# An embedding, mixer and expert tower on one core: the stretch between z and the experts rearranged, idle matmuls ahead of the h2n turns

## The chip, the cores and the metric

One NeuronCore of a Trainium2 chip runs the whole kernel in one launch. The metric is the device time of one execution in microseconds (us). TensorE (PE) multiplies and turns (transposes), VectorE (DVE), ScalarE (ACT) and GpSimd (POOL) do the elementwise work, SyncE (SP) issues most of the DMAs.

## The reference

```
h   = embed(x)                          # 32 x 128 ids, table 32000, four cutoffs, D = 256; ids outside give 0
n   = layernorm(h)
x1  = n @ w1.T + w1_b;  xc = silu(depthwise_conv3(x1))
y   = scan(xc): s = s*sigmoid(A) + xc*B;  y = sum(s*C) + D*xc      # 256 channels, 16 states, 128 steps
v   = silu(n @ v1.T + v1_b)
h2  = h + (y * v) @ w2.T + w2_b
n2  = layernorm(h2)
out = h2 + 0.5*shared(n2) + 0.25*(two experts of 8, chosen by token index)
shared(n2) = (silu(n2 @ sw1 + sb1) * (n2 @ sw3 + sb3)) @ sw2 + sb2
expert(n2) = gelu(n2 @ w1[e] + b1[e]) @ w2[e] + b2[e]
```

The expert ids are (11 t + 7919 k) mod 8 for token t, so tokens with the same t mod 8 share both experts.

## The kernel before

The kernel computes in fp32 accuracy with split operands: every matrix is kept as a rounded part (hi) and the remainder (lo), and `three` (L1171) issues three matmuls for one product. The hi half is a cast on ScalarE, the lo half a subtraction on VectorE or GpSimd. Each engine runs its own list of instructions in the written order, with semaphores between them.

Phase A embeds and normalizes 4096 tokens in four groups, projects them to x1 and v, and applies the convolution and silu; the result is turned by TensorE (`x_turn`), and `x_hi_part` (L828, ScalarE) and `x_lo_part` (L1030, VectorE) write the scan's input. The last of these tiles, group 3, u = 3, holds the channels from 128 on, and its turn is issued by TensorE behind q = 0 of the scan (L1264).

The scan is done as matmuls with Toeplitz matrices, 16 channels for each q in 0 to 15. For each q and each of two banks TensorE accumulates, ScalarE copies one part (L861), VectorE adds the other (L1067, `y_done`); TensorE's q waits for the y_done of q - 2. From q = 8 on y is also turned back, and `z_part` (VectorE, L1061) multiplies it into v: that is z. SyncE's Toeplitz loads run through the scan; behind them are queued the loads of h for slots 0 and 1 (`h_load`, into h_in) and the weight pieces (`piece_in(n)`). Pieces 0 to 8 are w2 (0), the experts of slot 0 (1: expert 7 into ex1, 8: expert 0 into ex0) and the six shared matrices sw (2 to 7). `piece_hi(n)` is ScalarE's half of a piece; the other is `piece_lo(n)` of VectorE (2 to 7) or of GpSimd (0, 8), and `first_expert_lo` of GpSimd for the two layers of piece 1.

Between z and the experts, for slot 0, in four groups g of 128 tokens:
- ScalarE makes zc_hi (`zc`, L868), GpSimd zc_lo (`mixer_lo`, L694), TensorE multiplies by w2 (`mixer_mm`);
- VectorE adds h (`mixer_out`, L1080), takes statistics (L985, L989) and adds eps (L994); GpSimd takes the power -1/2 (`power_step`, L563); VectorE writes the normalized h2n (`mixer_norm`, L998);
- TensorE turns h2n (`mixer_turn`, L1293), ScalarE and VectorE write h2nT_hi (L872) and h2nT_lo (L1094).

`add_w2_bias(par, ...)` (GpSimd, L735) adds the mixer's bias to the h of a slot before `mixer_out` uses it. `w2_bank` and `tr2_bank` name the PSUM banks of the mixer products and the turns.

The experts then run in eight slots, each of the 512 tokens with the same t mod 8. A slot has eight units (two of the old expert, four shared, two of the new one): `hidden` is the first layer (12 or 6 matmuls of 512 columns), `second` the second one (12 of 256 columns). Between units 1 and 4 of a slot lie the four `mixer_mm` of the next slot, between 3 and 6 its `mixer_turn`s. In slot 0 the shared units need VectorE's `w_lo_done[0]`: 4 pieces for the first hidden, 6 for the second layer. GpSimd waits for all 6 before it issues the load of the third expert (`expert_in(2, 0)`, L678) and goes into slot 0, whose first instruction is `mixer_lo(1, 0)`. SyncE issues piece 8 when `w_lo_done[1]` is 3, which is the second `first_expert_lo`.

Of the kernel before, what the change touches and what calls it, by code (L numbers as in the profile page):

```python
# [23 lines left out]
P = 128  # L24
# [51 lines left out]
def _tower(nc, ctx, ids, table, small, rows, w_a, w_b, w_e, kernel_rows, h_rows, out):  # L76
# [296 lines left out]
    def y_at(q, bank):  # L373
        first = q * CH + bank * CH // 2
        return y_sb[:, :, first:first + CH // 2]
# [8 lines left out]

    def w2_bank(e, g):

        return ps[(4, 5, 6, 4)[g] if isinstance(e, int) and e == 0 else 6]

    def z_cols(e, g):

# [23 lines left out]
    def _(sp):  # L414
# [9 lines left out]
        def h_load(e, par):  # L424
            sp.dma_start(h_in[:, par, :, :],
                         h_rows[bass.ds(e, 1), :, :, :].rearrange("o p g c -> (o p) g c")).then_inc(h_back[par], 16)
# [14 lines left out]
        def piece_in(n):  # L441
            raw, _, _, signal, _, _, _, src = PIECES[n]
            sp.dma_start(raw, src).then_inc(signal, 16)
# [57 lines left out]
        sp.dma_start(w2_bias, bass.AP(rows.tensor, 0, [[0, P], [D, 1], [1, D]])).then_inc(rows_in, 16)  # L501
        sp.wait_ge(ssm_done, 2 * (TRING - 3))
        h_load(0, 0)
        piece_in(1)
        piece_in(2)
        piece_in(3)
        h_load(1, 1)
        sp.wait_ge(ssm_done, 2 * NQ)
        for n in range(4, 8):
            piece_in(n)  # L510
# [23 lines left out]
    def _(pool):  # L534
# [213 lines left out]
        def first_expert_lo(layer):  # L748

            if layer == 0:  # L750
                pool.wait_ge(w_hi_done, 2)
            nc.gpsimd.tensor_tensor(ex1_lo[:, layer, :], stage[:, 2 + layer, :], f32(ex1_hi[:, layer, :]),
                                    ALU.subtract).then_inc(w_lo_done[1], 1)

        pool.wait_ge(rows_in, 48)
        add_w2_bias(0, 1)
        first_expert_lo(0)
        for g in range(GROUPS):
            mixer_lo(0, g)
        first_expert_lo(1)  # L760
        for g in range(GROUPS):
            power_step(g, g, eps2_done, rstd2_done)
        add_w2_bias(1, 1)
        pool.wait_ge(w_lo_done[0], LO_BY.count(0))
        expert_in(2, 0)
        slot(0, 0, 2)
# [8 lines left out]
    def _(act):  # L775
# [49 lines left out]
            need(act, hn_turned, 4 * i + pair + 1)  # L825
            nc.scalar.copy(hnT_at(hnT_hi, i, pair), hn_bank()).then_inc(hnT_hi_done, 1)

        def x_hi_part(i, u):  # L828
            need(act, x_turned, 4 * i + u + 1)
            nc.scalar.copy(x_at(x_hi, i, u), x_bank()).then_inc(x_hi_done, 1)  # L830

# [24 lines left out]
        run_phase_a(act, {"cat": cat_hi, "emb": h_out, "norm": norm, "hn": hn_hi, "x": x_hi_part, "out": out_, "silu": silu})  # L856

        for q in range(NQ):
            for bank in range(2):
                act.wait_ge(ssm_done, 2 * q + bank + 1)  # L860
                nc.scalar.copy(y_at(q, bank), y_part(q, bank, 1)).then_inc(y_low, 1)  # L861

        def zc(e, g):
            n = GROUPS * e + g
# [28 lines left out]
        def slot(e, par, ahead, before):  # L893
            for n in range(UNITS):
                if ahead and 1 <= n <= 4:
                    zc(e + 1, n - 1)
                if n == 6:

                    nc.scalar.activation(warm_out[:, 1:2], zero[:, :], ACT.Gelu)
                activate(e, n)  # L900
                if n or before:
                    hidden_hi(*((e, n - 1) if n else (e - 1, UNITS - 1)))
                if ahead and 3 <= n <= 6:
                    turn2_hi(e + 1, 1 - par, n - 3)

        piece_hi(1)
        for g in range(GROUPS):
            zc(0, g)
            if g < 2:
                piece_hi(2 + g)  # L910
        nc.scalar.activation(warm_out[:, 1:2], zero[:, :], ACT.Gelu)
        for g in range(GROUPS):
            turn2_hi(0, 0, g)
            piece_hi(4 + g)
        piece_hi(8)
        slot(0, 0, True, False)
        with act.Fori(0, 3) as i:
            slot(2 * i + 1, 1, True, True)
# [6 lines left out]
    def _(dve):  # L925
# [101 lines left out]
            nc.vector.tensor_tensor(hnT_at(hnT_lo, i, pair), hn_bank(), f32(hnT_at(hnT_hi, i, pair)),  # L1027
                                    ALU.subtract).then_inc(hnT_lo_done, 1)

        def x_lo_part(i, u):  # L1030
            need(dve, x_hi_done, 4 * i + u + 1)
            nc.vector.tensor_tensor(x_at(x_lo, i, u), x_bank(), x_at(x_hi, i, u), ALU.subtract).then_inc(x_lo_done, 1)

# [30 lines left out]
        for q in range(NQ):  # L1064
            for bank in range(2):
                dve.wait_ge(y_low, 2 * q + bank + 1)
                nc.vector.tensor_tensor(y_at(q, bank), y_part(q, bank, 0), y_at(q, bank), ALU.add).then_inc(y_done, 1)  # L1067
            if q > NQ // 2:
                z_part(q - NQ // 2 - 1)
        z_part(NQ // 2 - 1)  # L1070
# [68 lines left out]

        for u in range(8, 16):  # L1140
            z_part(u)
        piece_lo(2)
        piece_lo(3)
        for g in range(GROUPS):
            mixer_out(0, 0, g)
            if g >= 1:
# [3 lines left out]
                turn2_lo(0, 0, g - 2)  # L1150
        mixer_norm(0, 0, 3)
        turn2_lo(0, 0, 2)
        piece_lo(4)
        turn2_lo(0, 0, 3)
        piece_lo(5)
        piece_lo(6)
        piece_lo(7)
        slot(0, 0, True, False)
        slot(1, 1, True, True)
        slot(2, 0, True, True)  # L1160
# [9 lines left out]
    def _(pe):  # L1170
# [76 lines left out]
        for q in range(NQ):  # L1247
# [19 lines left out]
            if q >= NQ // 2:  # L1267
                if q == NQ // 2:
                    pe.wait_ge(y_done, NQ)
                y_turn(q - NQ // 2)  # L1270

        def mixer_mm(e, g):
            n = GROUPS * e + g
            need(pe, zc_lo_done, n + 1)
            if isinstance(e, int) and e == 0:
                need(pe, h2_done, g - 2)
            else:
                need(pe, h2_done, n)
            for k in range(HALVES):
                last = three(w2_bank(e, g)[:, 0:D], zc_hi[:, g, k, :], zc_lo[:, g, k, :],  # L1280
                             w2_hi[:, k, :], w2_lo[:, k, :], k == 0, k == HALVES - 1)
            last.then_inc(w2_done, 1)
# [88 lines left out]
        for g in range(GROUPS):  # L1371
            mixer_mm(0, g)
        for g in range(GROUPS):
            mixer_turn(0, g)
        slot(0, 0, True, False)
        with pe.Fori(0, 3) as i:
            slot(2 * i + 1, 1, True, True)
# [59 lines left out]
```

## Time and profile before

| what | value |
|---|---|
| runs shown | 441.69, 441.76, 440.62 us (median 441.69) |
| profiled execution | 440.82 us, span 439.0 us |
| mean granted clock of TensorE | 0.984 |
| busy | PE 400.8, PEld 351.4, DVE 275.9, ACT 243.4, POOL 212.7 us |
| scan on TensorE | 130 to 156.5 us of the span |
| z to the first matmul of slot 0 | 157 to 176.2 us |

Span is from the first to the last instruction. PE is TensorE's matmuls, PEld its weight loads, and the share of busy time is an average over all stages: TensorE is nearly full in the expert slots and half empty between 160 and 176 us.

### The profile page before, as it was taken

The numbers are of one execution on the slowest core, as the hardware profiler recorded it, in microseconds if no ns is written. First come the engines' busy times: TensorE is split into PE (matmuls) and PEld (weight loads), VectorE is DVE, ScalarE is ACT, GpSimd is POOL, SyncE is SP. The second block draws the span as 40 slices with busy tenths as digits, with TensorE's granted clock in tenths as the row PEclk, the third lists the DMA queues.
The fourth block names the chain that finished last, engine by engine and source line by source line (L and its number), as shares of the span: only waits on it lengthen the run. The fifth ranks groups of instructions, "written<-read, shape, count | busy, mean of one in ns | idle before, by whom it ended". The sixth has DMA issues, their size and how long they took to land.

```text
span 439.0 us, 8388 instructions
## 1 busy us (share of the span) xinstructions
PE 400.8 (91%) x2880; PEld 351.4 (80%) x2880; DVE 275.9 (63%) x607; ACT 243.4 (55%) x438; POOL 212.7 (48%) x237
## 2 busy tenths in 40 slices
PE   3879899899998883999999999999999999998996
PEld 2767788788678871788898988988988988887885
DVE  6667998889757689474565565565554654655333
ACT  4567878778876363635535635635635536535442
POOL 7678988831009166558337247247247336433000
PEclk9999999999999897799999999999999999999999
DMA  2533111299959962101111211201301301100101
GB/s 63 156 95 135 49 61 57 70 288 308 299 160 245 255 235 96 50 0 43 52 52 48 55 43 49 73 22 48 95 0 49 96 0 48 48 0 0 49 0 48
DMA packets 32779, 38.86 MB, mean 89 GB/s; under 512 B 3461, under 2 KB 29027, under 8 KB 32624
## 3 DMA queue, kind: packets, MB, share of 16 engines
q1 hardware_dynamic: 29616, 32.99, 24.1%
q0 software_dynamic: 3136, 5.52, 4.4%
q8 instruction: 15, 0.25, 0.2%
q14 instruction: 12, 0.10, 0.1%
HBM read 34.56 MB, written 8.65 MB: 98 GB/s over the span
## 4 chain that ended last, share of the span: by engine, by line
PE 69%; DVE 16%; ACT 6%; issue 5%; POOL 2%; DMA 1%; DVEq 0%; ACTq 0%; POOLq 0%
PE ps L1174 20%; PE ps L1175 20%; PE ps L1176 20%; DVE hid_lo L1107 3%; PE ps L1257 3%; DVE stat L985 2%; PE ps L1293 1%; DVE h2n L998 1%; PE ps L1212 1%; DVE v_sb L1061 1%; PE ps L1259 1%; PE ps L1182 1%; DVE catT_lo L978 1%; DVE act_out L1101 1%; DVE x_mid L1038 1%
## 5 line engine op out<-in xcount | busy, mean ns | idle before, releaser
L1107 DVE SCALAR_TENSOR_TENSOR hid_lo<-act_out,hid_hi 128x512 fp32r<-128x512 f32 x64 | 54.9, 859 | 58.9 <-ACT hid_hi L891 58.9
L878 ACT ACTIVATE act_out<-ps,vec 128x512 f32<-128x512 f32 x32 | 22.1, 689 | 89.7 <-PE ps L1176 89.7
L1101 DVE SCALAR_TENSOR_TENSOR act_out<-ps,vec,act_out 128x512 f32<-128x512 f32 x32 | 24.0, 751 | 53.7 <-ACT act_out L878 53.7
L701 POOL TENSOR_TENSOR h_sb<-h_sb,bias_e 128x256 f32<-128x256 f32 x32 | 24.3, 764 | 53.6 <-DVE h2n L998 53.6
L1176 PE MATMUL ps<-h2nT_hi,sw_lo 128*128 128x512 f32 x128 | 50.0, 391 | 0.0
L1175 PE MATMUL ps<-h2nT_lo,sw_hi 128*128 128x512 f32 x128 | 50.0, 391 | 0.0
L1174 PE MATMUL ps<-h2nT_hi,sw_hi 128*128 128x512 f32 x128 | 49.9, 390 | 0.0
L694 POOL TENSOR_TENSOR zc_lo<-v_sb,zc_hi 128x256 fp32r<-128x256 f32 x32 | 29.2, 912 | 36.5 <-ACT zc_hi L868 36.5
L882 ACT ACTIVATE act_out<-ps,vec 128x512 f32<-128x512 f32 x32 | 22.0, 689 | 41.2 <-PE ps L1176 41.0
L550 POOL DMA_INDIRECT cat<-table_dram,x_ids x32 | 36.6, 1144 | 8.4 <-issue 6.0
L891 ACT ACTIVATE hid_hi<-act_out 128x512 fp32r<-128x512 f32 x64 | 39.7, 622 | 0.0
L1174 PE MATMUL ps<-sw_hi,hid_hi 128*128 128x256 f32 x128 | 37.9, 296 | 1.2 <-DVE hid_lo L1107 1.2
L1174 PE MATMUL ps<-ex_hi,hid_hi 128*128 128x256 f32 x128 | 36.8, 288 | 1.2 <-DVE hid_lo L1107 1.2
L1176 PE MATMUL ps<-ex_hi,hid_lo 128*128 128x256 f32 x128 | 36.2, 283 | 0.0
L1175 PE MATMUL ps<-ex_lo,hid_hi 128*128 128x256 f32 x128 | 36.2, 283 | 0.0
L1176 PE MATMUL ps<-sw_hi,hid_lo 128*128 128x256 f32 x128 | 36.2, 283 | 0.0
L1175 PE MATMUL ps<-sw_lo,hid_hi 128*128 128x256 f32 x128 | 36.1, 282 | 0.0
L1174 PE MATMUL ps<-proj_hi,catT_hi 128*128 128x256 f32 x96 | 30.7, 320 | 3.2 <-DVE catT_lo L978 3.1
L563 POOL TENSOR_TENSOR rstd<-rstd,minus_half 128x1 f32<-128x1 f32 x32 | 18.2, 567 | 26.2 <-DVE rstd L994 25.9
L1176 PEld LDWEIGHTS ps<-h2nT_hi,sw_lo 128*128 128x128 f32 x128 | 24.0, 188 | 5.1
L1174 PE MATMUL ps<-hnT,wv_hi 128*128 128x512 f32 (+1 forms) x64 | 27.5, 430 | 0.6 <-DVE hnT L1027 0.3
L1175 PE MATMUL ps<-proj_lo,catT_hi 128*128 128x256 f32 x96 | 27.8, 290 | 0.0
(134 smaller groups left out, 1258.5 us busy)
## 6 DMA issues: line engine op xcount, KB each, us to landing
toep_l<-kernel_rows_dram SPq DMA_DIRECT2D x14, 512.0 KB, 7.3
toep_r<-kernel_rows_dram SPq DMA_DIRECT2D x12, 512.0 KB, 7.6
h_rows_dram<-h_ring SPq DMA_DIRECT2D x32, 128.0 KB, 2.2
h_in<-h_rows_dram SPq DMA_DIRECT2D x8, 512.0 KB, 4.4
stage<-w_e_dram POOLq DMA_DIRECT2D x7, 512.0 KB, 3.6
out_dram<-o_sb SPq DMA_DIRECT2D x7, 512.0 KB, 3.2
bias_e<-rows_dram SPq DMA_DIRECT2D x1, 1024.0 KB, 6.8
toep_r<-kernel_rows_dram SPq DMA_DIRECT2D x4, 256.0 KB, 6.0
```

The lines of the kernel that those rows point to most:

```text
L550: pool.indirect_dma_start(cat[:, r, :], None, table, bass.IndirectOffsetOnAxis(ap=x_ids[:, i, r:r + 1], axis=0), bounds_check=VOCAB - 1, o ...
L563: nc.gpsimd.tensor_tensor(rstd[:, m:m + 1], rstd[:, m:m + 1], minus_half[:, :], ALU.pow).then_inc(s_rstd, 1)
L694: nc.gpsimd.tensor_tensor(zc_lo[:, g, :, :], z_cols(e, g), f32(zc_hi[:, g, :, :]), ALU.subtract).then_inc(zc_lo_done, 1)
L701: nc.gpsimd.tensor_tensor(at, at, bias_e[:, bass.ds(e, 1), :].rearrange("p o c -> p (o c)"), ALU.add).then_inc(h2_biased, 1)
L878: nc.scalar.activation(act_out[:, n % 4, :], ps[bank][:, :], ACT.Silu, bias=vec[:, C_SB1 + j:C_SB1 + j + 1]).then_inc(act_done, 1)
L882: nc.scalar.activation(act_out[:, n % 4, :], ps[bank][:, :], ACT.Gelu, bias=vec[:, bass.ds(C_B1 + 2 * x + j, 1)]).then_inc(act_done, 1)
L891: nc.scalar.mul(hid_hi[:, n % 4, :], act_out[:, n % 4, :], 0.5 if kind == SHARED else 0.25).then_inc(hid_hi_done, 1)
L1101: nc.vector.scalar_tensor_tensor(act_out[:, n % 4, :], ps[bank + 1][:, :], vec[:, C_SB3 + j:C_SB3 + j + 1], act_out[:, n % 4, :], ALU.add, ...
L1107: nc.vector.scalar_tensor_tensor(hid_lo[:, n % 4, :], act_out[:, n % 4, :], 0.5 if kind == SHARED else 0.25, f32(hid_hi[:, n % 4, :]), ALU ...
L1174: nc.tensor.matmul(out_, hi, rhs_hi, start=start, stop=False, **kw)
L1175: nc.tensor.matmul(out_, hi, rhs_lo, start=False, stop=False, **kw)
L1176: return nc.tensor.matmul(out_, lo, rhs_hi, start=False, stop=stop, **kw)
```

## The change

The diff has six edits.

1. The last x tile's cast and subtraction (group 3, u = 3) move behind the y copies and adds of q = 1. ScalarE still waits for its turn ahead of q = 0.
2. SyncE loads h for slot 1 directly behind h for slot 0, ahead of pieces 1 to 3.
3. GpSimd: the second `add_w2_bias` moves from behind the powers to ahead of the four `mixer_lo`; both `first_expert_lo` move behind the fourth h2n.
4. VectorE: all six `piece_lo` move behind the last `turn2_lo` of slot 0. ScalarE: pieces 1 to 4 behind the four casts of the turns, 5 to 7 after them, piece 8 into unit 1 of slot 0.
5. The fourth mixer product of slot 0 gets bank 3 instead of 4, and TensorE's `mixer_mm` of slot 0 no longer waits for `h2_done`.
6. TensorE issues three 512-column matmuls whose result nobody reads ahead of each of the four turns, and three behind the last.

```diff
-        return ps[(4, 5, 6, 4)[g] if isinstance(e, int) and e == 0 else 6]
+        return ps[(4, 5, 6, 3)[g] if isinstance(e, int) and e == 0 else 6]
...
         h_load(0, 0)
+        h_load(1, 1)
         piece_in(1)
         piece_in(2)
         piece_in(3)
-        h_load(1, 1)
...
         add_w2_bias(0, 1)
-        first_expert_lo(0)
+        add_w2_bias(1, 1)
         for g in range(GROUPS):
             mixer_lo(0, g)
-        first_expert_lo(1)
         for g in range(GROUPS):
             power_step(g, g, eps2_done, rstd2_done)
-        add_w2_bias(1, 1)
+        pool.wait_ge(h2n_done, GROUPS)
+        first_expert_lo(0)
+        first_expert_lo(1)
...
         for q in range(NQ):
+            if q == 0:
+                act.wait_ge(x_turned, 4 * GROUPS)
             for bank in range(2):
                 act.wait_ge(ssm_done, 2 * q + bank + 1)
                 nc.scalar.copy(y_at(q, bank), y_part(q, bank, 1)).then_inc(y_low, 1)
+            if q == 1:
+                x_hi_part(GROUPS - 1, 3, last_one=True)
...
+                if n == 1 and isinstance(e, int) and e == 0:
+                    piece_hi(8)
+
-        piece_hi(1)
         for g in range(GROUPS):
             zc(0, g)
-            if g < 2:
-                piece_hi(2 + g)
         nc.scalar.activation(warm_out[:, 1:2], zero[:, :], ACT.Gelu)
         for g in range(GROUPS):
             turn2_hi(0, 0, g)
-            piece_hi(4 + g)
-        piece_hi(8)
+            piece_hi(1 + g)
+        for n in range(5, 8):
+            piece_hi(n)
         slot(0, 0, True, False)
...
+            if q == 1:
+                x_lo_part(GROUPS - 1, 3, last_one=True)
...
-        piece_lo(2)
-        piece_lo(3)
         for g in range(GROUPS):
             mixer_out(0, 0, g)
...
         turn2_lo(0, 0, 2)
-        piece_lo(4)
         turn2_lo(0, 0, 3)
-        piece_lo(5)
-        piece_lo(6)
-        piece_lo(7)
+        for n in range(2, 8):
+            piece_lo(n)
...
+        def keep_awake(times):
+
+            for _ in range(times):
+                nc.tensor.matmul(ps[2][:, :], w2_hi[:, 0, 0:P], w2_hi[:, :, :], start=True, stop=True)
+
         def mixer_mm(e, g):
             n = GROUPS * e + g
             need(pe, zc_lo_done, n + 1)
-            if isinstance(e, int) and e == 0:
-                need(pe, h2_done, g - 2)
-            else:
+            if not isinstance(e, int) or e:
                 need(pe, h2_done, n)
...
         for g in range(GROUPS):
+            keep_awake(3)
             mixer_turn(0, g)
+        keep_awake(3)
         slot(0, 0, True, False)
```

## Rows read from the trace of the kernel before

**Rows 1.** The profile's page: shares of the chain by engine; one group of DMA issues.
```profile
PE 69%; DVE 16%; ACT 6%; issue 5%; POOL 2%; DMA 1%; DVEq 0%; ACTq 0%; POOLq 0%
...
stage<-w_e_dram POOLq DMA_DIRECT2D x7, 512.0 KB, 3.6
```

**Rows 2.** Windows of 1 us: busy of PE, PEld, DVE, ACT, POOL; clock; DMA share; GB/s.
```profile
150.00:151.00 1.00, 1.00 (x12) 0.94 (x10) 0.88 (x4) 0.43 (x2) 0.00 (x0) 0.51 0.86 249
...
153.00:154.00 1.00, 1.00 (x26) 0.94 (x25) 0.86 (x2) 0.08 (x1) 0.00 (x0) 0.78 1.07 414
...
170.00:171.00 1.00, 0.00 (x0) 0.00 (x0) 0.97 (x4) 0.83 (x2) 0.32 (x1) 0.75 0.03 8
...
180.00:181.00 1.00, 1.00 (x4) 0.66 (x3) 0.00 (x0) 0.35 (x1) 0.56 (x1) 0.63 0.97 332
```

**Rows 3.** Timeline, scan stage: start us, us, instruction [idle before <-releaser].
```profile
133.56 0.19 PE L1257 MATMUL ps<-x_sb,toep_r 128*128 128x64 f16 x1 [0.77 <-DVE y_sb L1067]
...
131.78 0.59 ACT L830 CAST x_sb<-ps 128x512 f16<-128x512 f32 x1 [0.99 <-PE ps L1212]
...
132.26 1.21 ACT L861 COPY y_sb<-ps 128x256 f32<-128x256 f32 x4
...
132.40 0.69 DVE L1032 TENSOR_TENSOR x_sb<-ps,x_sb 128x512 f16<-128x512 f32 x1 [2.44 <-ACT x_sb L830]
...
148.46 0.18 PE L1259 MATMUL ps<-x_sb,toep_r 128*128 128x32 f16 x1 [1.87 <-issue]
```

**Rows 4.** Timeline of VectorE, 163 to 178 us.
```profile
163.26 2.42 DVE L1054 TENSOR_TENSOR sw_lo<-stage,sw_hi 128x512 fp32r<-128x512 f32 x2
165.60 0.41 DVE L1080 TENSOR_TENSOR h_sb<-ps,h_in 128x256 f32<-128x256 f32 x1
...
171.26 0.15 DVE L994 TENSOR_SCALAR rstd<-mv 128x1 f32<-128x1 f32 x1
...
172.07 2.42 DVE L998 TENSOR_SCALAR h2n<-h_sb,mv,rstd 128x256 f32<-128x256 f32 x1 [0.33 <-POOL rstd L563]
...
175.68 0.42 DVE L1094 TENSOR_TENSOR h2nT_lo<-ps,h2nT_hi 128x256 fp32r<-128x256 f32 x1 [0.25 <-ACT h2nT_hi L872]
176.02 1.88 DVE L1054 TENSOR_TENSOR sw_lo<-o_sb,sw_hi 128x512 fp32r<-128x512 f32 x3
```

**Rows 5.** Timeline of GpSimd, 155 to 182 us.
```profile
155.92 2.37 POOL L735 TENSOR_TENSOR h_in<-h_in,bias_row 128x1024 f32<-128x1024 f32 x1 [11.53 <-DMA h_in<-h_rows_dram]
...
164.12 1.00 POOL L694 TENSOR_TENSOR zc_lo<-v_sb,zc_hi 128x256 fp32r<-128x256 f32 x1 [0.29 <-ACT zc_hi L868]
...
171.49 0.55 POOL L563 TENSOR_TENSOR rstd<-rstd,minus_half 128x1 f32<-128x1 f32 x1 [1.17 <-DVE rstd L994]
172.00 2.34 POOL L735 TENSOR_TENSOR h_in<-h_in,bias_row 128x1024 f32<-128x1024 f32 x1
178.20 0.62 POOL L678 DMA_DIRECT2D stage<-w_e_dram  x1 [3.86 <-DVE sw_lo L1054]
180.44 0.87 POOL L694 TENSOR_TENSOR zc_lo<-v_sb,zc_hi 128x256 fp32r<-128x256 f32 x1 [1.62 <-ACT zc_hi L868]
```

**Rows 6.** Timeline of TensorE, 166 to 183 us.
```profile
166.16 0.36 PE L1174 MATMUL ps<-w_hi,zc_hi 128*128 128x256 f32 x1 [1.29 <-DVE h_sb L1080]
...
176.16 0.79 PE L1174 MATMUL ps<-h2nT_hi,ex_hi 128*128 128x512 f32 x1 [0.92 <-DVE h2nT_lo L1094]
...
181.37 0.39 PE L1174 MATMUL ps<-w_hi,zc_hi 128*128 128x256 f32 x1
...
182.18 0.39 PE L1174 MATMUL ps<-h2nT_hi,sw_hi 128*128 128x512 f32 x1
...
182.41 0.40 PE L1175 MATMUL ps<-h2nT_lo,sw_hi 128*128 128x512 f32 x1
```

**Rows 7.** VectorE's halves of pieces by source: ns min/median/max, first and last start.
```profile
L1054 DVE TENSOR_TENSOR sw_lo<-o_sb,sw_hi x4: 676/682/686, 174.7 to 177.2; 128x512 fp32r<-128x512 f32 x4
L1054 DVE TENSOR_TENSOR sw_lo<-stage,sw_hi x2: 1136/1250/1364, 163.3 to 164.3; 128x512 fp32r<-128x512 f32 x2
```

More of the change, by code:

```diff
@@ L826, in hn_hi, with x_hi_part @@
             nc.scalar.copy(hnT_at(hnT_hi, i, pair), hn_bank()).then_inc(hnT_hi_done, 1)
-        def x_hi_part(i, u):
+        def x_hi_part(i, u, last_one=False):
+            if isinstance(i, int) and i == GROUPS - 1 and u == 3 and not last_one:
+                return
             need(act, x_turned, 4 * i + u + 1)
@@ L1028, in hn_lo, with x_lo_part @@
                                     ALU.subtract).then_inc(hnT_lo_done, 1)
-        def x_lo_part(i, u):
+        def x_lo_part(i, u, last_one=False):
+            if isinstance(i, int) and i == GROUPS - 1 and u == 3 and not last_one:
+                return
             need(dve, x_hi_done, 4 * i + u + 1)
```

## The prediction

> **What bounds the kernel now.** The page first: 69% of the chain that ended last is TensorE, 16% VectorE, 6% ScalarE [rows 1]. Most of the kernel is TensorE-bound expert slots, and the change leaves those alone. It works on the three stretches where TensorE is not the bound, so I read the trace in order of time there.
>
> At the start of the scan, TensorE stands idle 0.77 us before its first matmul of q = 2, released by VectorE's y_sb add [rows 3]. Ahead of that add lie ScalarE's x_hi cast (131.78, 0.59 us) and VectorE's x_lo (132.40, 0.69 us) of the last x tile.
>
> From 163 to 176 us VectorE sets the pace. It does two piece halves in 2.42 us, then starts the first mixer add at 165.60, is still at its eps(3) at 171.26, and then its last h2n, an instruction with a tile of 128x256, takes 2.42 us [rows 4]. GpSimd's bias add (172.00, 2.34 us) lies over exactly that stretch [rows 5]. A piece half costs 0.68 us by itself and 1.14 or 1.36 us beside GpSimd's work [rows 7].
>
> From 176.16 TensorE runs twelve matmuls of slot 0 at the low clock: they take until 181.37, where the next two of that width are 0.23 us apart (182.18, 182.41) [rows 6]. The clock fell to half within 170 to 171 us and rose within 180 to 181 us, and an earlier fall lasted from 150 to inside 153 us, after 1.87 us in which TensorE issued nothing [rows 2, 3].
>
> **The change part by part.** I count in the times of the trace before; the gain of the scan's start is taken off at the end.
>
> *Scan start.* The x cast and its subtraction go behind the copies of q = 0 and 1. The first y copy can start at 131.78 in place of 132.26, and the first add no longer stands behind x_lo, which ended at 133.09 [rows 3]. Copy 0.37 us and add 0.42 us (estimates from 1.21 us for four overlapping copies [rows 3] and the 0.41 us of a 128x256 add [rows 4]) give y_done at about 132.6, ahead of 132.8, where TensorE wanted it (133.56 - 0.77). The moved pair costs 0.59 + 0.69 us behind q = 1, under adds that TensorE needs only two q later. Gain 0.77 us if the later stalls keep their length, 0 if they swallow it; I take 0.77, since TensorE's share is 1.00 in the windows at 150 and 153 us, so it works without slack behind it [rows 2].
>
> *Mixer start.* Without the two pieces VectorE's first mixer add moves from 165.60 to 163.3, a gain of 2.3 us. Not all of it is kept: the first power must now wait for GpSimd's last zc_lo (164.12 + 1.00 = 165.12), so power (0.55 us) and h2n(0) come at 165.75, where the old cadence from 163.3 had asked for about 165.3: 0.45 us lost [rows 4, 5]. The fourth mixer matmul no longer waits for an add to free its bank. From the first add to eps(3) were 5.66 us (171.26 - 165.60). So eps(3) comes at 163.3 + 5.66 + 0.45 = 169.4.
>
> *Last h2n.* Before, eps(3) at 171.26 was followed by the power (171.49, 0.55 us) and h2n from 172.07 to 174.49 [rows 4, 5]. GpSimd now has nothing to do between the last power and h2n_done, so h2n costs about 0.40 us (estimate: the add of the same tile takes 0.41), and it ends at 169.4 + 0.81 + 0.40 = 170.6. From its end to the end of the last h2nT_lo were 1.61 us (174.49 to 175.68 + 0.42) [rows 4]; slot 0 starts at 172.3 in place of 176.16. I take 172.1 to 172.3; 3.9 us gained here. GpSimd's first expert half (estimate 1.3 us for 512 columns, between the 0.87 of 256 and the 2.37 of 1024 [rows 5]) starts at 170.65 and is done at 171.95, just in time for the first matmul.
>
> *Idle matmuls.* Five groups of three 512-column matmuls, 0.23 us each at full clock [rows 6]: 0.7 us a group, 1.3 us at half clock. The h2n turns come every 1.4 to 1.5 us (5.66 us for four), so a group fits between two; only the first, right behind the mixer matmuls, can hold a turn, by 0.3 to 0.4 us, and ScalarE and VectorE have that much slack there. The last group lies beside the 1.61 us of turn, cast and subtraction. Cost 0, at most 0.4 us. In return TensorE is idle for no more than 0.8 us at a time up to slot 0; before, it idled 1.29 us ahead of 166.16 [rows 6] and the clock did not fall until 170 us, after three turns with nothing between them. So I expect full clock up to slot 0.
>
> *Bias add and load order.* GpSimd does two adds of 2.37 us ahead of zc_lo(0): 155.92 to 160.6, where zc_lo(0) started at about 160.5 before. The four zc_lo end no later than 165.1, since the last waits for ScalarE anyway [rows 5]. Cost 0 to 0.3 us; if h_load(1, 1), which is now second in the queue, landed only at 160, it would be 1 us.
>
> *Pieces behind.* Here the gain is given back in part. VectorE now has six halves behind the last h2nT_lo where it had three in 1.88 us [rows 4]; GpSimd waits for all six (it waited 3.86 us for the last of them before), then issues its DMA (0.62 us) and only then makes zc_lo of slot 1 (0.87 us), which the mixer matmul in slot 0 needs [rows 5]. Six halves at a cadence of 0.63 us are 3.8 us; the second expert half on GpSimd (about 1.3 us) lies over the first of them, and by the price beside GpSimd that costs 0.6 us [rows 7]. So from 171.95: last half 176.4, DMA issue 176.7 to 177.3 (0.30 us later, as before), zc_lo to 178.2, matmul at 178.2 in place of 181.37 (where zc_lo also ended only at 181.31). TensorE's twelve matmuls in front of it last 2.75 us at full clock, to 174.9. It then stands idle for 3.3 us. Bounds: halves at 0.63 us without any collision 177.6; all at 1.25 us 181.9 [rows 7]. Net gain at this point: 3.2 us.
>
> The expert load of piece 8 leaves later too, behind GpSimd's second half, at about 173.4. With a landing after 3.6 us [rows 1], ScalarE splits it until about 178.1, ahead of the next activation that TensorE's third group needs (178.2 + 0.8 + 2.75). It stays hidden up to some 3 us of delay.
>
> A half beside GpSimd takes nearly twice its time [rows 7], and the one-input h2n waited for nearly the whole add [rows 4, 5]. The Trainium skill (GPSIMD Engine Reference, Specifications) says that GpSimd's SBUF interfaces are shared with VectorE, with contention for instructions in a two-port mode or with two SBUF inputs. By that rule the new order moves a collision from h2n to the first piece half; without a rule of this kind the sum would come out 0.6 us lower, with it as above. The trace agrees.
>
> *The clock after the gap.* 1.87 us of idle TensorE came ahead of a fall that lasted 3.4 us: four windows of 1 us, the first at 0.51 and the last at 0.78 [rows 2, 3], with about half lost in each of the first three and 0.22 in the last, are 1.7 us of full-clock work. The new gap of 3.3 us is nearly twice as long. TensorE is the bound behind it (the shared groups follow one another), so a fall costs about 1.7 us of time; 0 if it doesn't come, 2.5 us if it is like the second, where twelve matmuls took 5.2 in place of 2.75 us [rows 6].
>
> **The sum.** The profiled execution took 440.82 us (span 439.0, and 1.8 around it). 440.8 - 0.8 (scan) - 3.2 (slot 0) + 1.7 (clock) = 438.5. The median of the runs shown is 441.69 and they run from 440.62 to 441.76, so the profiled one is at their lower end; I add 0.4, half the distance: 438.9.
>
> **Rivals.**
> 1. *The clock holds through the gap.* For it: it was full at 165 to 167 us in spite of gaps. Against: once, 1.87 us came ahead of a fall [rows 3]. 438.9 - 1.7 = 437.2.
> 2. *The new gate in slot 0 eats it all (slower).* Place: the mixer matmul of slot 1 behind the first twelve matmuls. If all six halves run at 1.25 us [rows 7], they end at 179.45 and the matmul comes at 181.3, as before; TensorE then idled over 6 us, and the clock falls as the second time, 2.5 us: 440.8 + 2.5 + 0.4 = 443.7, or 442.9 if the scan's 0.8 are kept. It decides from a matmul later than about 180, a half over 1.05 us on average. For it: both halves beside GpSimd were that slow. Against: GpSimd has a single instruction left to run beside them, then waits for them itself.
> 3. *The gain is largely swallowed, no change.* The scan's issue stalls (1.87 us at 146.6 [rows 3]) grow when TensorE comes earlier, h_load lands late, the clock falls for longer: -0.8 becomes 0, -3.2 becomes -2.5, +1.7 becomes +2.5, 441.2 with the 0.4.
>
> **How the numbers follow.** Forecast 0.50, clock holds 0.27, no change 0.15, slower 0.08. A measurement here can tell about 0.3% (1.3 us) from no change: faster is below 440.4, slower above 443.0. The forecast's own range is 437.8 to 440.2; with rival 1 and most of rival 3 the range is 436.5 to 441.3. Faster: 0.50 + 0.27 + a little of rival 3, 0.80; within 0.3% 0.14; slower 0.06.
>
> **What would show it.** TensorE's idle before q = 2 gone; the first mixer add near 162.5, slot 0's first matmul near 171.4 (both with the 0.8 off); no h2n over 0.5 us before slot 0; full clock from 154 us to slot 0; the mixer matmul in slot 0 after about 3.3 us of idle TensorE, released by GpSimd's zc_lo, and a half clock for some 3.4 us around it. Wrong if that matmul comes less than 1.5 us behind the twelfth, or if the clock is low in the stretch of turns, or if the scan ends no earlier.

## The result and the profile after

The changed kernel takes 439.55 us (median of 20 runs, 436.82 to 440.99), the kernel before 441.27 us (20 runs, 440.05 to 443.61). The ratio of the two kernels is 0.995, 95% interval 0.9931 to 0.9969: 2.2 us less, between 1.4 and 3.0 (the two medians are 1.7 us apart). The profiled execution took 438.76 us.

The page of the changed kernel: its span, the clock by slices, the chain's shares and the group of zc_lo subtractions.

```profile
span 437.0 us, 8419 instructions
...
PEclk9999999999999989999999999999999999999999
...
PE 67%; DVE 15%; ACT 5%; issue 5%; DMA 3%; POOL 3%; DVEq 0%; ACTq 0%; POOLq 0%; SPq 0%
...
L694 POOL TENSOR_TENSOR zc_lo<-v_sb,zc_hi 128x256 fp32r<-128x256 f32 x32 | 29.5, 921 | 33.4 <-ACT zc_hi L875 33.3
```

Against [rows 1], DMA's share of the chain has gone from 1% to 3% and POOL's from 2% to 3%, and in the clock line one dip stands in the slice around 158 us where there were two dips, around 148 and from 165 to 187.

The scan's idle ahead of q = 2 is gone: no row of TensorE with idle time stands between 130 and 135 us. What stands there later are three waits with no releaser (timeline of TensorE):

```profile
141.10 0.20 PE L1266 MATMUL ps<-x_sb,toep_l 128*128 128x32 f16 x1 [1.29 <-issue]
...
148.09 0.18 PE L1266 MATMUL ps<-x_sb,toep_r 128*128 128x32 f16 x1 [1.60 <-issue]
...
156.14 0.18 PE L1266 MATMUL ps<-x_sb,toep_l 128*128 128x32 f16 x1 [1.92 <-issue]
```

In this document such a wait is called a stall. Before, the same three stalls were 0.66, 1.87 and 0.39 us, the second of them in [rows 3]; the other two are these:

```profile
141.21 0.21 PE L1259 MATMUL ps<-x_sb,toep_l 128*128 128x32 f16 x1 [0.66 <-issue]
...
155.72 0.18 PE L1259 MATMUL ps<-x_sb,toep_l 128*128 128x32 f16 x1 [0.39 <-issue]
```

Now they are 1.29, 1.60 and 1.92. That is 1.9 us more than before, and the scan's last copies by ScalarE are 0.4 us later (first line before, second line now), not 0.8 us earlier.

```profile
156.53 0.37 ACT L861 COPY y_sb<-ps 128x256 f32<-128x256 f32 x1 [0.16 <-PE ps L1259]
...
156.95 0.37 ACT L866 COPY y_sb<-ps 128x256 f32<-128x256 f32 x1 [0.16 <-PE ps L1266]
```

VectorE from the first mixer add to the last piece half, to be held against [rows 4]:

```profile
164.29 0.41 DVE L1091 TENSOR_TENSOR h_sb<-ps,h_in 128x256 f32<-128x256 f32 x1
...
170.25 0.15 DVE L1001 TENSOR_SCALAR rstd<-mv 128x1 f32<-128x1 f32 x1
...
171.07 0.41 DVE L1005 TENSOR_SCALAR h2n<-h_sb,mv,rstd 128x256 f32<-128x256 f32 x1 [0.33 <-POOL rstd L563]
...
172.42 0.42 DVE L1105 TENSOR_TENSOR h2nT_lo<-ps,h2nT_hi 128x256 fp32r<-128x256 f32 x1 [0.60 <-ACT h2nT_hi L879]
172.76 2.38 DVE L1063 TENSOR_TENSOR sw_lo<-stage,sw_hi 128x512 fp32r<-128x512 f32 x2
175.07 2.48 DVE L1063 TENSOR_TENSOR sw_lo<-o_sb,sw_hi 128x512 fp32r<-128x512 f32 x4
```

The mixer add follows z at once (164.29; z itself ended 1.0 us later than before, when it ended at 163.26), the last h2n takes 0.41 in place of 2.42 us, and the six halves take from 172.76 to 177.55. GpSimd, against [rows 5]: both bias adds at the front, the two expert halves as one row of 3.04 us (1.28 and 1.80), and the DMA issue and zc_lo of slot 1 only behind VectorE's last half.

```profile
156.66 4.69 POOL L735 TENSOR_TENSOR h_in<-h_in,bias_row 128x1024 f32<-128x1024 f32 x2 [12.30 <-DMA h_in<-h_rows_dram]
...
165.15 0.90 POOL L694 TENSOR_TENSOR zc_lo<-v_sb,zc_hi 128x256 fp32r<-128x256 f32 x1 [0.28 <-ACT zc_hi L875]
166.00 0.56 POOL L563 TENSOR_TENSOR rstd<-rstd,minus_half 128x1 f32<-128x1 f32 x1
...
171.56 3.04 POOL L752 TENSOR_TENSOR ex_lo<-stage,ex_hi 128x512 fp32r<-128x512 f32 x2 [0.53 <-DVE h2n L1005]
177.85 0.62 POOL L678 DMA_DIRECT2D stage<-w_e_dram  x1 [3.25 <-DVE sw_lo L1063]
178.50 0.86 POOL L694 TENSOR_TENSOR zc_lo<-v_sb,zc_hi 128x256 fp32r<-128x256 f32 x1
```

TensorE, against [rows 6]. Slot 0 starts at 172.98; its twelfth matmul starts at 175.56, and the next instruction, 3.46 us of idle later, is released by zc_lo:

```profile
170.18 0.44 PE L1303 MATMUL ps<-ident,h2n 128*128 128x128 f32 x2 [0.56 <-DVE h2n L1005]
...
172.98 0.47 PE L1181 MATMUL ps<-h2nT_hi,ex_hi 128*128 128x512 f32 x1 [0.31 <-POOL ex_lo L752]
...
175.56 0.39 PE L1183 MATMUL ps<-h2nT_hi,ex_lo 128*128 128x512 f32 x1
179.41 0.38 PE L1181 MATMUL ps<-w_hi,zc_hi 128*128 128x256 f32 x1 [3.46 <-POOL zc_lo L694]
```

The clock in three stretches (windows: busy of PE, PEld, DVE, ACT, POOL, then the clock, DMA share, GB/s): low while z is turned (before, the same four microseconds were at 1.00), full among the turns of h2n, and full through the idle stretch in this execution.

```profile
157.00:161.00 4.00, 3.71 (x21) 3.33 (x20) 3.55 (x7) 0.76 (x2) 4.00 (x2) 0.57 0.92 306
169.00:173.00 4.00, 2.92 (x14) 1.55 (x12) 3.00 (x11) 3.03 (x8) 2.31 (x4) 1.00 0.01 2
176.00:179.00 3.00, 0.00 (x0) 0.00 (x0) 2.15 (x4) 2.33 (x4) 1.13 (x2) 1.00 0.82 325
```

The mean granted clock differs between the 20 executions: six had 0.996 (mean 437.8 us), three 0.992 (439.0 us), eleven 0.986 or 0.988 (440.2 us). The profiled one is of the first kind. The mean doesn't say where in an execution the clock was low; the profiled one had its fall at 157 us.

### The profile page after: what moved, and what is told of

Its sections match the earlier page's. It is cut to its first block, busy times and chain, and to the rows that moved or that the text cites. A ratio compares the mean times of both kernels' runs of the same rounds, so it can differ in the third digit from the quotient of the medians.

```text
span 437.0 us, 8419 instructions
## 1 busy us (share of the span) xinstructions
PE 401.4 (92%) x2895; PEld 352.5 (81%) x2895; DVE 273.8 (63%) x607; ACT 243.1 (56%) x438; POOL 212.0 (49%) x237
## 3 DMA queue, kind: packets, MB, share of 16 engines
HBM read 34.56 MB, written 8.65 MB: 99 GB/s over the span
## 4 chain that ended last, share of the span: by engine, by line
PE 67%; DVE 15%; ACT 5%; issue 5%; DMA 3%; POOL 3%; DVEq 0%; ACTq 0%; POOLq 0%; SPq 0%
PE ps L1181 20%; PE ps L1182 19%; PE ps L1183 19%; DVE hid_lo L1118 3%; DMA toep_l<-kernel_rows_dram 2%; PE ps L1264 2%; PE ps L1303 1%; DVE stat L992 1%; PE ps L1219 1%; PE ps L1189 1%; DVE sw_lo L1063 1%; DVE catT_lo L985 1%; DVE x_mid L1047 1%; DVE act_out L1112 1%; ACT act_out L885 1%
## 5 line engine op out<-in xcount | busy, mean ns | idle before, releaser
L1183 PE MATMUL ps<-proj_hi,catT_lo 128*128 128x256 f32 x96 | 27.9, 290 | 0.0
```

Of the source, the lines that this page charges most:

```text
L1183: return nc.tensor.matmul(out_, lo, rhs_hi, start=False, stop=stop, **kw)
```

## Experiments

Each was timed against runs of the kernel before on the same chip; its ratio to that kernel is what is compared, since the medians of before lie between 441.0 and 442.3 us.

### e1_gate: GpSimd goes into slot 0 without waiting for VectorE's six halves

```diff
-        pool.wait_ge(w_lo_done[0], LO_BY.count(0))
-        expert_in(2, 0)
         slot(0, 0, 2)
...
             for g in range(2):
                 mixer_lo(1, g)
+                if g == 0:
+                    pool.wait_ge(w_lo_done[0], 2)
+                    expert_in(2, 0)
                 mixer_bias(0, 0, g)
```

> The changed kernel, with one wait of GpSimd moved: it goes into slot 0 with zc_lo of slot 1 at once, and only behind it waits, for 2 of VectorE's piece halves (those of the buffer to be overwritten) in place of all 6, and issues the load of the third expert. Theory (the gate gave back a part of the gain): in the changed kernel TensorE idled 3.46 us ahead of the mixer matmul at 179.41, released by zc_lo. Now zc_lo follows zc_hi (ended 175.90) and the matmul comes about 1.0 us behind the twelfth; 2.4 us less, and about 0.4 to 1.7 us more on average where the clock no longer falls behind the gap: 436 to 437 us against 439.5. Rival (another wait stands right behind, the shared pieces that VectorE halves until 177.5, or ScalarE's wait for piece 8): the idle only moves to the next group and the time is within 0.5 us of the changed kernel, 439 to 440.

Measured 436.71 us (5 runs), ratio 0.9888 (0.9871 to 0.9904). TensorE's first and thirteenth instruction of slot 0:

```profile
173.13 0.47 PE L1182 MATMUL ps<-h2nT_hi,ex_hi 128*128 128x512 f32 x1 [0.31 <-DVE h2nT_lo L1106]
...
177.26 0.39 PE L1182 MATMUL ps<-w_hi,zc_hi 128*128 128x256 f32 x1 [1.15 <-POOL zc_lo L694]
```

The idle stretch is 1.15 us in place of 3.46, and all executions had a mean clock of 0.994 to 0.996. The gate is what it was said to be: in the profiles the mixer matmul stands 12.8 us after the end of z in place of 15.1. It cost the changed kernel about 2.7 us (ratios 0.995 and 0.9888, with 1.1 us of uncertainty). The edit moves the wait behind the first zc_lo and also lowers it from six halves to two; which of the two does more was not separated.

### e2_no_awake: without the fifteen idle matmuls

```diff
         for g in range(GROUPS):
-            keep_awake(3)
             mixer_turn(0, g)
-        keep_awake(3)
```

> The changed kernel without its fifteen idle matmuls. Theory (what they save lies in the shadow of the gate): the clock falls between 169 and 173 us, slot 0's first twelve matmuls take 4 to 5.2 us in place of 2.75, to about 178, but the mixer matmul waits for zc_lo until 179.4 anyway; time within 1 us of the changed kernel (438.5 to 440.5). Rival (the prediction's own step taken alone: the idle matmuls are worth the 2.5 us of the low clock): 441.5 to 442.

Measured 438.20 us, ratio 0.9942 (0.9929 to 0.9955): no slower than the changed kernel, and a little below the range expected. The clock falls among the turns and is back before the mixer matmul (windows, then TensorE's first and thirteenth instruction):

```profile
169.00:176.00 7.00, 5.16 (x14) 3.65 (x14) 5.82 (x11) 4.58 (x9) 3.05 (x3) 0.51 0.31 108
176.00:181.00 5.00, 3.61 (x19) 2.78 (x18) 2.68 (x6) 4.03 (x6) 3.57 (x5) 1.00 0.47 165
```

```profile
171.80 0.79 PE L1181 MATMUL ps<-h2nT_hi,ex_hi 128*128 128x512 f32 x1 [0.92 <-DVE h2nT_lo L1105]
...
178.13 0.39 PE L1181 MATMUL ps<-w_hi,zc_hi 128*128 128x256 f32 x1 [1.39 <-POOL zc_lo L694]
```

Slot 0's twelve matmuls run mostly at half clock and fill the time in which the full clock of the changed kernel only waits: the idle stretch is 1.39 us. The matmul behind it stands 15.2 us after the end of z here (162.9) and 15.1 in the changed kernel (164.3).

### e5_gate_no_awake: both edits

> e1_gate without the fifteen idle matmuls. In e2_no_awake leaving them out cost nothing while the gate stood (438.2 us). Theory (they are worth something only where nothing else holds TensorE behind them): with the gate moved, the twelve matmuls at half clock end about 2.5 us later than in e1_gate, the mixer matmul follows at once, and the time is 1.3 to 2.5 us above e1_gate's 436.7: 438 to 439. Rival (they are worth nothing anywhere, since ScalarE's and GpSimd's chain zc_hi, zc_lo shifts with the first activation and the clock is regained sooner): 436.2 to 437.2.

Measured 437.32 us, ratio 0.9911 (0.9888 to 0.9933), against 0.9888 of e1_gate: 1.0 us more, with intervals that overlap a little. The profiles say the same. The mixer matmul has no idle time ahead of it here:

```profile
178.33 0.39 PE L1182 MATMUL ps<-w_hi,zc_hi 128*128 128x256 f32 x1
```

It stands 14.2 us after the end of z (164.2), where e1_gate has 12.8; the spans are 436.3 and 435.1 us. So with the gate gone the idle matmuls save 1.3 us up to that point, in the one profile of each kernel; the runs put their worth at about 1 us and don't exclude nought.

### e6_fill: thirteen more idle matmuls in the gap

```diff
+                if n == 1 and isinstance(e, int) and e == 0:
+                    keep_awake(13)
                 if ahead and 1 <= n <= 4:
                     mixer_mm(e + 1, n - 1)
```

> The changed kernel with thirteen more idle 512-column matmuls in slot 0, ahead of the mixer matmul that waits for zc_lo: they fill 3.0 of the 3.46 us in which TensorE idled. The gate stays where it was. Theory (in most executions of the changed kernel the clock falls behind this gap: their mean granted clock lies between 0.986 and 0.996, and those at 0.996 take 436.8 to 438.9 us, those at 0.986 to 0.988 take 439.3 to 441.0): the mean clock stays at 0.992 or more in all executions, and the median is 437.5 to 438.2, 1.5 us below the changed kernel. Rival (the falls that cost are those of the scan, and slot 0's costs nothing): 439 to 440 us with clocks spread as before.

Measured 438.08 us, ratio 0.9932 (0.991 to 0.9953), six executions with clocks of 0.991 to 0.996. TensorE in the gap:

```profile
173.86 3.16 PE L1282 MATMUL ps<-w_hi 128*128 128x512 f32 x13
177.46 0.38 PE L1181 MATMUL ps<-w_hi,zc_hi 128*128 128x256 f32 x1 [0.45 <-POOL zc_lo L694]
```

The gate is as late as ever and no useful work was added, yet the lowest mean clocks (0.986 and 0.988) are gone. By medians (438.08 and 439.55) this is worth 1.5 us, by ratios 0.8, and the two intervals overlap. The changed kernel's own executions spread over more: 437.8 us at its highest mean clock, 440.2 at its lowest.

### e3_scan_only and e7_scan_undone: the scan's edit alone, and the change without it

> The kernel before with one edit of the change: the last x tile's cast and subtraction behind the copies and adds of q = 1. Theory (the scan is paced by its issue stalls, which take back what is gained ahead of them): TensorE's idle of 0.77 us before q = 2 is gone, the stalls in the scan grow by about as much (they were 0.66, 1.87 and 0.39 us before, and longer by 0.9 to 1.6 us in the changed kernel), the scan's last matmul ends within 0.5 us of 156.5, and the time is that of before within 0.5 us. Rival (the 0.77 us are kept): scan ends near 155.7 and the time is 0.8 us less.

Measured 440.92 us (12 runs), ratio 1.0002 (0.9988 to 1.0016). The idle before q = 2 was gone, and the three stalls were 1.84, 1.40 and 0.70 us: 3.94 in place of 2.92. The profiled execution has the same span as before, 439.0 us.

> The changed kernel with the last x tile's cast and subtraction back in their old place. Theory (the scan's issue stalls take back what the edit gains, as in e3_scan_only): TensorE's 0.77 us of idle before q = 2 is back and the stalls sum to about 3 us in place of 4.81; the median is that of the changed kernel within 0.5 us (439.0 to 440.0). Rival (the edit gives its 0.77 us here): 440.2 to 440.5 us.

Measured 439.77 us (12 runs), ratio 0.9972 (0.9954 to 0.9989), which overlaps the changed kernel's. The idle of 0.77 us was back, and the stalls 0.66 and 2.15 us, 2.81 in all. So the edit gives nothing that can be told, alone or in the change: what is gained ahead of the first stall goes into the stalls.

This profile shows what the changed kernel's own does not, the fall of the clock behind the gap (TensorE's mixer matmul, then windows):

```profile
177.75 0.58 PE L1171 MATMUL ps<-w_hi,zc_hi 128*128 128x256 f32 x1 [3.40 <-POOL zc_lo L694]
```

```profile
169.00:176.00 7.00, 4.80 (x20) 3.02 (x18) 6.07 (x11) 5.80 (x11) 3.40 (x3) 1.00 0.28 98
176.00:184.00 8.00, 6.25 (x20) 5.25 (x21) 1.67 (x5) 2.88 (x3) 7.21 (x8) 0.57 0.32 114
```

The clock is full through the turns with their idle matmuls, and 0.57 over the eight microseconds from 176, that is some 6.9 us at half clock. TensorE is still idle in the first 1.75 of them, where a low clock costs nothing. What a fall here costs can be read from the mixer matmul to the end of the span. That stretch is 257.6 us in the profiles of before, the changed kernel, e2, e3 and e6, all without a low clock in it. It is 260.2 us here (2.5 more), and 259.2 to 259.3 us (1.6 to 1.7 more) in those of e4, e9, e10 and e11, where the clock was 0.79 over the 8 us from the mixer matmul. The idle time ahead of these falls was 1.8 to 3.4 us; in the changed kernel's profile 3.46 us brought none.

### e9_shift: 24 turns of the identity ahead of the scan

```diff
         pe.wait_ge(h_done, RES * GROUPS)
+        for _ in range(24):
+            nc.tensor.transpose(ps[2][:, 0:P], ident[:, :], ident[:, :])
```

> The changed kernel with 24 turns of the identity more on TensorE in front of the scan (their result is not read): 48 more instructions of TensorE and about 2.7 us. The stalls of the scan without a releaser stood at the same matmul of q = 7, 11 and 15 in the kernel before, in the changed kernel and in three variants with the same instructions ahead of them. Theory (they are waits for TensorE's own instructions, which come in fixed pieces by DMA): each stall now stands 48 instructions earlier in the scan. Rival (they are waits for the scan's data or for buffers): each stall stands at the same matmul as before.

One execution, 443.39 us. Counted over the rows of the scan's 512 matmuls, the stalls of the changed kernel stand in front of the 270th, 384th and 494th, and those of the other twelve profiles stand at the same places (the third where there is one). Here they are in front of the 246th, 360th and 475th: 24, 24 and 19 earlier, where 24 turns with their weight loads had been put in.

```profile
142.64 0.18 PE L1268 MATMUL ps<-x_sb,toep_l 128*128 128x32 f16 x1 [1.14 <-issue]
...
149.77 0.18 PE L1268 MATMUL ps<-x_sb,toep_r 128*128 128x32 f16 x1 [0.90 <-issue]
...
158.26 0.22 PE L1266 MATMUL ps<-x_sb,toep_l 128*128 128x64 f16 x1 [3.10 <-issue]
```

They go with the instructions, not with the data, and not with the time either, since they come 1.5 to 2.1 us later than in the changed kernel (and 0.4 to 1.0 us earlier if one counts from the scan's first matmul, which the turns put back by 2.5 us). The Trainium skill (Runtime: NRT & Kernel Launch, Instruction fetch mechanics) has a sequencer fetch its instructions by DMA in blocks of 256. The trace agrees. In the changed kernel's profile, from the first stall to the second and from the second to the third, the matmuls and weight loads (first two counts) are these:

```profile
141.10:148.09 6.99, 5.39 (x126) 5.31 (x127) 4.12 (x9) 2.61 (x7) 2.95 (x4) 1.00 1.03 237
148.09:156.14 8.05, 5.89 (x127) 5.57 (x126) 5.30 (x11) 2.61 (x7) 0.00 (x0) 1.00 1.03 300
```

That is 253 recorded instructions both times. The Trainium skill calls the cost mostly hidden (same section), and here it was 0.2 to 3.5 us where it showed.

### e10_loads_late and e12_held: fewer bytes on the DMA engines in the scan

> The changed kernel with the loads of h and of pieces 1 to 3 (2 MB) held back until the scan's last matmul. Theory (the scan's stalls, which e9_shift showed to move with the instructions, are long because the DMA engines are full): the first, at 141 us, ahead of these loads, stays at 0.7 to 1.8 us; the third, at 154 to 156 us, is under 0.5 us; the scan ends 1 to 2 us earlier. h arrives about 3 us later than before and the whole takes 2 us or more longer. Rival (the stalls don't depend on these loads): third stall of 0.4 to 1.9 us as before.

One execution, 445.37 us. The stalls were 2.13 and 1.08 us, and there was no third. DMA share (last but one column) in the stretch of the first and ahead of the absent one:

```profile
140.00:145.00 5.00, 2.87 (x59) 2.84 (x59) 1.70 (x4) 1.49 (x4) 4.19 (x6) 0.91 1.05 243
...
150.00:155.00 5.00, 5.00 (x116) 5.00 (x115) 4.28 (x9) 2.61 (x7) 0.00 (x0) 1.00 0.58 147
```

> e8_gate_zc with the loads of pieces 1 to 3 (1 MB) held back until the scan's last matmul; h of both slots is loaded where it was. In e10_loads_late, with h held back too, the third stall was gone, and all came 3 us later for want of h. Theory (the third stall is a price of the DMA load that these pieces are a part of, and the pieces are not needed before 168 us): the third stall is under 0.5 us in the profile, and the time is 0.3 to 1 us below e8_gate_zc's 436.5: 435.5 to 436.2. Rival (the h loads and the Toeplitz loads alone keep the DMA engines full until 155 us, or the stalls' sum stays and only moves to the second): 436.2 to 437.0.

```diff
         h_load(1, 1)
-        piece_in(1)
-        piece_in(2)
-        piece_in(3)
         sp.wait_ge(ssm_done, 2 * NQ)
-        for n in range(4, 8):
+        for n in range(1, 8):
```

(the rest is e8_gate_zc)

Measured 436.85 us (4 runs), ratio 0.9882 (0.9846 to 0.9919), the same as e8_gate_zc. Again there is no third stall, but the other two took 4.97 us:

```profile
142.03 0.20 PE L1266 MATMUL ps<-x_sb,toep_l 128*128 128x32 f16 x1 [2.67 <-issue]
...
150.76 0.18 PE L1266 MATMUL ps<-x_sb,toep_r 128*128 128x32 f16 x1 [2.30 <-issue]
```

The absent third stall proves little, though: the profiles of e1_gate, e4_bias_back, e7_scan_undone and e8_gate_zc lack it too, with all loads in place. The scan of e10_loads_late was 1.0 us shorter than the changed kernel's, as its theory had it, but so was that of e6_fill with all loads in place (25.8 us each, 26.8 in the changed kernel). Over the fourteen profiles the first stall varies from 0.66 to 2.67 us and the second from 0.67 to 3.52. The two with the x tile in its old place have the smallest sums, 2.92 and 2.81 us; the twelve with the edit have 3.15 to 5.14. The first stall shows it best. Counted from the scan's first matmul, TensorE came to it after 10.5 us in the two profiles with the x tile in its old place, and after 9.7 us in the eleven others that have no turns ahead: the edit's 0.8 us has arrived there. The wait ended after 11.2 us in the two, and after 10.8 to 12.4 us (median 11.3) in the eleven. So the gain is gone behind the first stall, as if the instructions came at their own time. That the load of the DMA engines makes the stalls long is not shown, and what sets their lengths stays open. For e12_held the rival held: the time did not fall.

### e4_bias_back: the second bias add back behind the powers

```diff
         add_w2_bias(0, 1)
-        add_w2_bias(1, 1)
...
             power_step(g, g, eps2_done, rstd2_done)
+        add_w2_bias(1, 1)
```

> The changed kernel with the second add_w2_bias of GpSimd put back behind the four powers. Theory (the port shared by VectorE and GpSimd made the last h2n long): the fourth h2n takes about 2.4 us in place of 0.41, slot 0 starts 2.0 us or more later, both expert halves of GpSimd start 2.3 us later, and the mixer matmul behind the gate comes 2 to 2.5 us later; 441.5 to 442 us, the changed kernel's gain gone. Rival (the gate takes it up: VectorE's six halves, not GpSimd, set it, and the collision only moves): less than 1 us more than the changed kernel, 439.5 to 440.5.

Measured 441.36 us (12 runs), ratio 1.0008 (0.9995 to 1.0021). VectorE's last h2n, and GpSimd's add beside it:

```profile
170.40 2.43 DVE L1005 TENSOR_SCALAR h2n<-h_sb,mv,rstd 128x256 f32<-128x256 f32 x1 [0.33 <-POOL rstd L563]
```

```profile
170.33 2.35 POOL L735 TENSOR_TENSOR h_in<-h_in,bias_row 128x1024 f32<-128x1024 f32 x1
```

The h2n is as long as before, and the mixer matmul behind the gate stands 17.1 us after the end of z in place of 15.1. The clock also fell behind the gate's 1.82 us of idle time in this profile (above). With this one move undone, the rest of the change gives nothing that can be told.

### e11_pieces_first: two halves back ahead of the first mixer add

```diff
+        piece_lo(2)
+        piece_lo(3)
         for g in range(GROUPS):
             mixer_out(0, 0, g)
...
-        for n in range(2, 8):
+        for n in range(4, 8):
             piece_lo(n)
```

(with ScalarE's piece_hi(1) to (3) among the first casts, as before)

> The changed kernel with pieces 2 and 3 of VectorE (and ScalarE's casts 1 to 3) back ahead of the first mixer add, nothing else. Theory (most of what the mixer start gains by the move is given back at the gate, where two halves less stand then): slot 0's first matmul comes about 1.9 us later, but the mixer matmul behind the gate only 0.5 to 1 us later, after 2.4 us of idle in place of 3.46; 439.5 to 440.5 us. Rival (the move is worth its 2.3 us as the first mixer add shows them): 441.3 to 442.

Measured 439.88 us (12 runs), ratio 0.9969 (0.9944 to 0.9994); overlaps the changed kernel's. TensorE's first and thirteenth instruction of slot 0, z having ended at 165.24:

```profile
176.00 0.47 PE L1184 MATMUL ps<-h2nT_hi,ex_hi 128*128 128x512 f32 x1 [0.32 <-POOL ex_lo L752]
...
181.22 0.39 PE L1184 MATMUL ps<-w_hi,zc_hi 128*128 128x256 f32 x1 [2.22 <-POOL zc_lo L694]
```

One of the last four halves took 1.79 us beside GpSimd, the other three 0.68. From the end of z slot 0 starts 2.1 us later than in the changed kernel (10.8 and 8.7), but the mixer matmul only 0.9 us later (16.0 and 15.1), after 2.22 us of idle. More than half of what the piece move gains is given back at the gate.

### e8_gate_zc: zc_hi of slot 1 earlier on ScalarE as well

```diff
+            if g == 3:
+                zc(1, 0)
             piece_hi(1 + g)
```

(and not again in unit 1 of slot 0; the rest is e1_gate)

> e1_gate with one cast of ScalarE moved: zc_hi of slot 1's first group comes behind the fourth turn's cast, ahead of the last four piece casts, in place of behind slot 0's first activation. Theory (what was left of the gate in e1_gate is the chain activation, zc_hi, zc_lo, 1.15 us of idle TensorE): zc_lo follows GpSimd's second expert half, the mixer matmul comes right behind the twelfth; the next wait, for the shared pieces of VectorE, takes back up to 0.5 us. 0.5 to 1.1 us below e1_gate's 436.7: 435.6 to 436.2. Rival (GpSimd beside VectorE's halves slows them by as much): within 0.3 us of e1_gate.

Measured 436.51 us, ratio 0.9886 (0.9862 to 0.9909), as e1_gate. The mixer matmul now comes without idle time, and the next wait stands one group later, for VectorE's shared pieces:

```profile
177.71 0.50 PE L1184 MATMUL ps<-h2nT_hi,sw_hi 128*128 128x512 f32 x1 [0.92 <-DVE sw_lo L1066]
```

GpSimd's zc_lo and bias add beside VectorE's last four halves stretch them to 3.95 us, against 2.48 in the changed kernel: the rival held. (In e1_gate they took 3.89.) e1_gate, e8_gate_zc and e12_held, which can't be told apart, are the best kernels of this study: 436.5 to 436.9 us, a ratio of 0.988 to 0.989.

Two edits of the change were run only with the others: the order of the h loads, and the bank of the fourth mixer product. Of the second, the profile shows that TensorE's wait of 1.29 us for VectorE's add [rows 6] is gone and the fourth product waits 0.20 us for zc_lo.

## Why the prediction was right, and where not

*Size.* Forecast 438.9 us from a start of 441.2 (profiled 440.8 and 0.4): 2.3 us less. Measured 2.2 us less (1.4 to 3.0). The terms did not all come out, and that the total did is in part luck (see *The sum*).

*Scan start (0.8 us).* The idle time went as computed, the gain did not arrive. The step that failed is "since TensorE's share is 1.00 in the windows at 150 and 153 us, so it works without slack behind it". Between those windows it stalls at fixed places in its own instruction list (e9), and an earlier TensorE waits longer there (e3, e7). The term is 0, which had been given as the other bound; rival 3 had the reason, stalls that grow when TensorE comes earlier. One of the prediction's own signs of being wrong, "if the scan ends no earlier", came true: it ended 0.4 us later. So the first mixer add stood at 164.29 and slot 0's first matmul at 172.98, where 162.5 and 171.4 had been named, and the clock was not full from 154 us on but 0.57 from 157 to 161, behind the third stall.

*Mixer start.* The first add follows z at once, as forecast. From the first add to eps(3) were 5.96 us (forecast 6.11, before 5.66): the power waits for the last zc_lo, which costs 0.3 us where 0.45 had been said.

*Last h2n.* 0.41 us, forecast 0.40, and e4 shows its cause. First matmul of slot 0 after the end of z: 8.7 us, forecast 8.9 (172.2 - 163.3); 0.31 us of it was the wait for GpSimd's first expert half, called "just in time".

*The gate.* Six halves took 4.8 us (forecast 4.5: the two beside GpSimd 2.38 us, the other four 2.48), idle time 3.46 us (3.3), mixer matmul 15.1 us after z (14.9). Before it was 18.1 (181.37 - 163.3): the term of 3.2 measured 3.0. By the forecast's own terms the last h2nT_lo ends at 172.2, so the halves could not begin at 171.95; they did begin about as soon after z as was said (8.5 us, forecast 8.65), since the mixer start cost less. e1_gate shows that this wait held TensorE, and that most of the time won there is kept. Rival 2, halves of 1.25 us throughout, came true only as the mean of the two beside GpSimd: one took 0.68 us, the other 1.79.

*Idle matmuls.* They kept the clock full among the turns, as said, and cost nothing. What the prediction did not say is that they also bring nothing here: a matmul that ends 2.5 us earlier ends in front of the gate. e2_no_awake is as fast.

*The clock after the gap (1.7 us, 0.50 against 0.27).* Judged by the mean clocks it fell in some executions and not in others: 6 of 20 have the highest mean clock, among them the profiled one, which looks like rival 1 at slot 0. Its 438.76 us is not rival 1's 437.2, nor 436.8 (without the 0.4 added for the median): z ended 1.0 us later than before in place of 0.8 earlier, and slot 0 gave 3.0 in place of 3.2. Where a fall came, 1.6 to 2.5 us were lost behind the mixer matmul (e7 and four other profiles), so the price of 1.7 was about right for one that comes. As an average over executions the best figures are the 0.8 to 1.5 us that filling the gap brings (e6); how often the fall comes in the changed kernel was not seen in a profile of it.

*The sum.* Over all executions -0.8 became 0 and -3.2 became -3.0, and the clock term of +1.7 came out at some +0.8 to +1.5. In sum 1.5 to 2.2 us less by the parts. The miss at the scan is hidden in the total by a clock term that was too high.

The two profiled executions show it more plainly. Their scans start at 130.02 and 130.07 us. The end of z is 1.0 us later: 0.4 at the end of the scan, by the stalls, and 0.6 while z is turned, at the low clock behind the third. (From the scan's last matmul to the end of z are 6.85 us in the eleven profiles at full clock there, and 7.47 in this one.) The mixer matmul comes 3.0 us sooner after z, and behind it both take 257.6 us. That is -2.0, the difference of the spans (439.0 and 437.0), where the forecast had -0.8, -3.2 and +1.7, or -2.3. Two errors of 1.8 and 1.7 us cancel.

## What to carry to other kernels

When work is moved behind a stage to start it earlier, look up who waits for the last of that work: here a single conservative wait of GpSimd (for six halves, where two were enough) gave back about 2.7 us of what the move had gained, and moving and lowering that wait mended it. Idle matmuls that hold the clock are worth something only where TensorE is the bound right behind them (nothing with the gate, about 1 us without it), and a clock kept full only to reach a wait sooner makes the idle stretch longer. Before counting an early gain, look for waits with no releaser behind it: here the first one took all of 0.8 us back, though TensorE was fully busy in the windows that had been looked at.

## What the runs showed of the hardware

- TensorE stood idle with no releaser for 0.2 to 3.5 us, two or three times in a scan, at places 253 recorded instructions apart that moved with the number of its instructions ahead. In the eleven profiles with the scan's edit and no turns ahead of it the first such wait took 1.03, 1.3, 1.58, 1.84, 2.13 or 2.67 us, some 0.27 us apart or twice that; why was not looked into.
- A VectorE subtraction with both inputs in SBUF took 0.68 us by itself and 1.14 to 1.79 us when it was slowed beside a GpSimd subtraction; an h2n of 0.41 us took 2.43 us beside a GpSimd add of 2.35 us, so it gained nothing from starting beside it.
- Behind 3.4 us of idle TensorE the clock fell in the profile of e7_scan_undone and did not in that of the changed kernel (3.46 us). A fall that did come there cost 1.6 to 2.5 us. Within the 20 executions of the changed kernel the mean granted clock went from 0.986 to 0.996, and the groups with the lowest and the highest differ by 2.4 us in mean time.
